# The last expert layer: eight lower-half splits go from GpSimd to VectorE, the gathers come in one run, and the combines come later

## The reference

```
scores = softmax(x_n @ gate_w.T)
i1, i2 = the two experts with the best scores
e(x)   = (silu(x @ W1[e].T) * (x @ W3[e].T)) @ W2[e].T
x     += scores[i1] * e_i1(x_n) + scores[i2] * e_i2(x_n) + shared(x_n)
```

## Time and profile before

| | |
|---|---|
| median of three runs | 1633.42 us |
| the profiled execution | 1632.18 us, its span 1630.4 us |
| TensorE busy | 1563.6 us, 96% of the span |
| VectorE, ScalarE, GpSimd busy | 1244.6, 1213.4, 1161.1 us |
| granted TensorE clock, mean | 0.993 of full speed |

### The profile page before, as it was taken

The page is one execution under the profiler, slowest core; times in us unless marked ns, Lnnn a source line. Parts: engine busy times, 40 slices in busy tenths (PEclk is TensorE's granted clock), DMA queues, the critical chain, the costliest instruction groups (busy, mean ns, idle before and its releaser), DMA issues. The chain is left out here.

```text
span 1630.4 us, 26805 instructions
## 1 busy us (share of the span) xinstructions
PE 1563.6 (96%) x9214; PEld 908.7 (56%) x9214; DVE 1244.6 (76%) x2330; ACT 1213.4 (74%) x1904; POOL 1161.1 (71%) x817
## 2 busy tenths in 40 slices
PE   3998899999999999999999999999999999998898
PEld 2565445555555555555555555555567566677665
DVE  7878787777777777777777777778787787977637
ACT  7876888988988989988988888887564543344442
POOL 0865888888888888888888898887565232556344
PEclk9999999999999999999999999999999999999999
DMA  9312879889779879879889788888103420000522
GB/s 307 126 53 47 135 145 166 151 144 185 147 145 184 150 145 179 151 151 173 149 152 170 146 144 156 156 147 145 32 1 76 113 55 1 1 1 14 114 95 84
DMA packets 641355, 197.10 MB, mean 121 GB/s; under 512 B 601531, under 2 KB 639046, under 8 KB 640966
## 3 DMA queue, kind: packets, MB, share of 16 engines
q1 hardware_dynamic: 636646, 188.19, 59.5%
q0 software_dynamic: 1536, 4.20, 0.8%
q10 hardware_dynamic: 3040, 3.02, 0.5%
HBM read 36.71 MB, written 10.22 MB: 29 GB/s over the span
## 5 line engine op out<-in xcount | busy, mean ns | idle before, releaser
L967 POOL TENSOR_TENSOR Pl<-Pm,Ph 128x1024 f16<-128x1024 f32 x256 | 545.5, 2131 | 44.4 <-ACT Ph L1308 43.9
L1298 ACT ACTIVATE Pm<-banks,nbias,s_scale 128x1024 f32<-128x1024 f32 x256 | 307.4, 1201 | 96.5 <-DVE nbias L1924 95.5
L1922 DVE TENSOR_REDUCE nmax<-banks 128x1 f32<-128x1024 f32 x256 | 311.6, 1217 | 87.3 <-PE banks L2454 86.9
L1308 ACT ACTIVATE Ph<-Pm 128x1024 f16<-128x1024 f32 x256 | 268.1, 1047 | 1.5
L946 POOL TENSOR_TENSOR rp_b<-rp_s,rope 128x512 f32<-128x512 f32 x128 | 162.8, 1272 | 98.4 <-ACT rp_s L1275 96.7
L1955 DVE SCALAR_TENSOR_TENSOR X<-banks,rinv,X 128x256 f32<-128x256 f32 x256 | 112.2, 478 | 113.2 <-PE banks L2454 113.2
L2452 PE MATMUL banks<-QK_hi 128*128 128x512 f16 x512 | 194.1, 379 | 1.6 <-DVE QK_lo L2013 0.9
L2452 PE MATMUL banks<-PT_hi,V_hi 128*128 128x512 f16 x512 | 194.0, 379 | 0.3 <-DMA PT_lo<-Pl 0.3
L2453 PE MATMUL banks<-QK_lo,QK_hi 128*128 128x512 f16 x512 | 194.0, 379 | 0.0
L2454 PE MATMUL banks<-QK_hi,QK_lo 128*128 128x512 f16 x512 | 194.0, 379 | 0.0
L2454 PE MATMUL banks<-PT_hi,V_lo 128*128 128x512 f16 x512 | 194.0, 379 | 0.0
(11 more groups left out here) (318 smaller groups left out, 3968.2 us busy)
## 6 DMA issues: line engine op xcount, KB each, us to landing
moe_raw<-in_L_ffn_W SPq DMA_DIRECT2D x48, 128.0 KB, 2.5
w_all<-in_L_attn_w_qkv SPq DMA_DIRECT2D x3, 2048.0 KB, 15.8
a_raw<-in_L_attn_w_qkv SPq DMA_DIRECT2D x24, 256.0 KB, 3.2
PT_hi<-Ph SPq DMA_TRANSPOSE x256, 3.4
PT_lo<-Pl SPq DMA_TRANSPOSE x256, 3.3
xs<-zeros SPq DMA_DIRECT2D x1, 2944.0 KB, 17.0
yd<-y_sb ACTq DMA_DIRECT2D x5, 512.0 KB, 2.9
raw_gu<-in_L_ffn_w_gate_up SPq DMA_DIRECT2D x2, 1024.0 KB, 7.2
```

The source lines that it names most:

```text
L967: nc.gpsimd.tensor_tensor(Pl[:, z % 4, :], Pm[:, k, :], Ph[:, z % 4, :], ALU.subtract).then_inc(pl_done.sem, 1)
L1298: nc.scalar.activation(Pm[:, k, :], two_banks[z % 2][:], ACT.Exp, bias=nbias[:, z:z + 1], scale=s_scale[:], accum_out=rsum[:, z:z + 1]).th ...
L1308: nc.scalar.activation(Ph[:, z % 4, :], Pm[:, (base * SLOTS + z) % 3, :], copy).then_inc(ph_done.sem, 1)
L1922: nc.vector.tensor_reduce(nmax[:, z:z + 1], two_banks[z % 2][:], AX, ALU.max, negate=True).then_inc(max_done.sem, 1)
```

## The change

Three tables and one loop are changed; no instruction computes anything else than before.

- `LO_BY_POOL` was 5 to 24 (20 units). It is now 5 to 12 and 21 to 24 (12 units). The lo of units 13 to 20 is now made by VectorE.
- The 16 gathers stood in pairs behind the lo of units 13 to 20. They now stand in one run behind the lo of unit 12 (`POOL_BEFORE_GATHER = 8`), ahead of the lo of unit 21.
- The combine of tile t stood in iteration 16+t. It now stands in iteration 19+t for tiles 0 to 5, and the combines of tiles 6 and 7 both stand in iteration 25.

```diff
-    COMBINE_AT = {16 + t: (t,) for t in range(TT)}
-    GATHER_BEHIND = {13 + t: (t,) for t in range(TT)}
-    LO_BY_POOL = tuple(range(5, NUB - 1))
+    COMBINE_AT = {19: (0,), 20: (1,), 21: (2,), 22: (3,), 23: (4,), 24: (5,), 25: (6, 7)}
+    LO_BY_POOL = (5, 6, 7, 8, 9, 10, 11, 12, 21, 22, 23, 24)
+    POOL_BEFORE_GATHER = 8
...
-                for i in LO_BY_POOL:
-                    expert_lo(i)
-                    gather(GATHER_BEHIND.get(i, ()))
+                expert_lo(LO_BY_POOL[:POOL_BEFORE_GATHER])
+                for i in range(2):
+                    pool.wait_ge(y_in[i].sem, 16 * XG // 2)
+                for t in range(TT):
+                    for k in range(TOPK):
+                        nc.gpsimd.indirect_dma_start(yg[:, t, k, :], None, yd,
+                                                     bass.IndirectOffsetOnAxis(pos[:, k, t:t + 1], 0)).then_inc(yg_in[t // 2].sem, 16)
+                expert_lo(LO_BY_POOL[POOL_BEFORE_GATHER:])
```

More of the change, by code:

```diff
@@ L1084, in scatter, with expert_lo @@
                         nc.gpsimd.indirect_dma_start(xs, bass.IndirectOffsetOnAxis(pos[:, k, t:t + 1], 0), row_tile(t), None).then_inc(xs_in.sem, 16)
[L1086 to L1099, removed]
+            def expert_lo(units):
+                for i in units:
+                    n = width(i)
+                    pool.wait_ge(mo_hi_done.sem, mo_hi_done.in_head(1, i + 1))
+                    nc.gpsimd.tensor_tensor(bT_lo[:, i % MT, 0:n], bo_h[:, i % 2, 0:n], bT_hi[:, i % MT, 0:n], ALU.subtract).then_inc(lo_pool.sem, 1)
             def last_experts(l):
```

## The result

The changed kernel took 1646.91 us (median of 4 runs, 1645.60 to 1647.91), the kernel before 1633.43 us beside it (4 runs, 1632.18 to 1634.13). The ratio is 1.0083 with a 95% interval of 1.0065 to 1.0100: 13.5 us or 0.83% slower, where I had forecast 1634.5 us and no change. The profiled execution took 1646.39 us with a span of 1644.3 us, 13.9 us more than before.

The account below looks back on a forecast made before the run. TensorE was taken to bound the kernel until 1622 us, then VectorE's lo(25) and adds. Terms 0 + 0 + 1.04 + 0 = +1.04 us on the median of 1633.42 gave 1634.5 us, range 1632.0 to 1636.8.

Parts of the forecast that it names:

- The gathers in one run: Sixteen gathers on GpSimd, from about 1575 to 1596 us, then some 10 us idle ahead of lo(21); worth zero.
- Both signs of being wrong: TensorE waiting for a lo or an add before 1620 us, or a span growing by more than 2 us.
- The third rival: Sixteen gathers in a row choke on GpSimd, lo(21) comes late, TensorE stands still 5.3 us: 1639.8 us; chance 3 in 100.
- The lo on VectorE: Lo of units 13 to 20 on VectorE, 0.61 us each in iterations 14 to 21; costs nothing.
- the margin of 0.06 us: VectorE in iterations 19 to 21, with lo and combine: 3.84 us of work in a period of 3.90.
- the cover of 1.3 us: Time to spare before TensorE waits for drained banks, with a lo ahead of the adds; hides an overrun of 1.3 us.
- the rule of the Trainium skill: A two-SBUF-input VectorE instruction and a GpSimd SBUF read share an interface; the later waits. Run might end 3.4 us later.
- The combines three iterations later: Zero up to tile 5; tiles 6 and 7 between product 25 and lo(25) on VectorE delay the end by 1.04 us.
- The sum: All terms for the span together: 0 + 0 + 1.04 + 0 = +1.04 us, from 1630.4 to 1631.4 us.
- the term of the combines: Combines of tiles 6 and 7 ahead of lo(25) on VectorE: +1.04 us, twelve adds following without a gap.

Follow-up runs that it names:

- e15: Changed kernel with a GpSimd pause of about 1.05 us ahead of the gathers of tiles 2, 4 and 6 only: 1634.56 us against 1633.27 before, ratio 1.0006.
- e9: Changed kernel, its run of sixteen gathers fetching and combining 64 of 128 rows each: 1647.20 us in one run.
- e8: Kernel before with a GpSimd pause of about 1 us ahead of each tile's two scatters but the first tile's: 1638.43 us against 1633.72, ratio 1.0032.
- e11: Kernel before with one more dense unit ahead of the sorted ones and a GpSimd pause behind every four scatters: 1630.05 us, ratio 0.9981.
- e1: Changed kernel with its gathers waiting in pairs for the upper halves of units 13 to 20: 1634.70 us against 1633.37 before, ratio 1.0007.
- e14: Changed kernel with a GpSimd pause of about 1.05 us ahead of each pair of gathers from the second tile on: 1635.04 us, ratio 1.0007.
- e4: Kernel before with the late combines alone and nothing else of the change: 1634.99 us against 1633.37, ratio 1.0011.
- e5: Changed kernel with its gathers in two groups of eight, behind the upper halves of units 13 and 17: 1636.01 us in one run, before 1633.72.
- e7: Changed kernel, its run of sixteen gathers fetching 128 of 256 columns, half the bytes: 1645.89 us in one run.

## Why the prediction was wrong

The gathers in one run: this step failed. I wrote that GpSimd is idle behind the run "and the long run delays nobody", and "This part is worth zero". The gathers themselves came as forecast (the first at 1575.32, about 1 us earlier than before; the last one done at 1595.1, forecast 1595.8), and the part cost 12 to 13 us. GpSimd was idle for 23 us ahead of lo(21) instead of 10, since lo(21) became due 12 us later. Both signs of being wrong that I had named came: TensorE waited 7.4 us for a lo before 1620 us, and the span grew by 13.9 us. I had asked who is queued behind the run on GpSimd, and who waits for the data. I had not asked what else the run goes past, and TensorE's signals were held up by it. The cost is not in the number of DMAs: with pauses the same sixteen cost nothing that shows (e15), and with half the rows each they cost as much as in the changed kernel (e9).

The third rival had the right sign and the right trigger, at 3 chances in 100, and the wrong mechanism. It let the gathers themselves slow down, with a threshold of 2.27 us each. They kept to 1.24 to 1.29 us, while TensorE stood still.

Against it I had set "twelve scatters in one run kept 1.26 to 1.46". That row is true, and it was the wrong question to it: I looked at how long the scatters took, not at what the others did beside them. The windows of 1516 to 1528 us and the two "remote" waits stood in the trace that I had. TensorE was idle there for 1.24 + 2.08 + 1.33 = 4.65 us. At most 3.41 of these belong to it: the first 1.24 us, a wait for VectorE, are there in e8 and e11 as well, although updates are prompt at that place.

The lo on VectorE: right that it costs nothing. In e1, with all of them, TensorE is busy for the whole of both windows. But the margin of 0.06 us did not hold in iteration 21, timeline of VectorE in the changed kernel:

```profile
1616.79 0.75 DVE L2277 SCALAR_TENSOR_TENSOR bo_h<-banks,l_pow,bo_s 128x512 f32<-128x512 f32 x1
...
1618.06 1.77 DVE L2260 SCALAR_TENSOR_TENSOR X<-yg,wk,X 128x256 f32<-128x256 f32 x2
...
1621.33 0.73 DVE L2277 SCALAR_TENSOR_TENSOR bo_h<-banks,l_pow,bo_s 128x512 f32<-128x512 f32 x1
```

Beside lo(21) on GpSimd (1618.29) the combine took 1.77 us instead of 1.00, and the iteration 4.54 us instead of 3.90. The 0.64 us were within the cover of 1.3 us, and the next iteration made them up (product 23 at 1624.59, two periods behind product 21).

I had weighed the rule of the Trainium skill, page "SBUF — State Buffer", section "Who interferes with whom", against the change. It cost nothing here: in the changed kernel no gather began while a lo was running, and they kept their 0.95 us. Where one does, the trace agrees with the rule. In e14 (GpSimd, then VectorE):

```profile
1587.74 1.38 POOL L1119 DMA_INDIRECT yg<-yd,pos  x1 [0.19 <-issue]
```

```profile
1587.55 0.68 DVE L2299 TENSOR_TENSOR bT_lo<-bo_h,bT_hi 128x512 f16<-128x512 f32 x1
```

The gather began with 0.49 us of the lo left and took 0.42 us longer than its neighbour (0.96 us).

The combines three iterations later: right. I had +1.04; e4 and the changed kernel both show 1.05 in the trace, and e1, which is the change without the long run, has 1634.70 us and a span of 1631.5, where I had forecast 1634.5 and 1631.4.

The sum therefore lacked one term, +12.1 us up to product 25: 10.07 us of TensorE standing still, and 2.0 us in its work around that. Most of the latter is the half clock: TensorE worked under it from 1599.49 to 1602.6, which costs an estimated 1.6 us (half of 3.1). Another 0.66 us come from the half clock at the end, behind a wait of TensorE of 2.1 us for an add; e1 and e4, with the same combines, have their twelve adds without a gap, so this is no part of the term of the combines.

## What to carry to other kernels

Before putting DMAs of GpSimd into one long run, look at what the other engines do beside the longest run that the trace already has. Where the waits name "remote", "an unknown queue" or "issue" on an engine that ought to wait for TensorE, compare the end of the matmul with the start of its waiter. Runs of four with 1 us of other work of GpSimd between were enough here beside the gathers, provided that nobody needs the data sooner; beside the last four scatters of e11 they were not quite enough.

## What the runs showed of the hardware

- TensorE's semaphore updates are late beside a run of indirect DMAs that GpSimd issues every 1.26 us. The first late one belongs to a matmul that ended 5.0 to 6.8 us after the run began, beside the fifth or sixth DMA (changed kernel 6.45, scatters of before 6.3, the groups of e5 6.8 and 5.0). Updates then come in order, up to 13 us late (changed kernel), and the last ones in a burst 0.8 to 3.5 us after GpSimd is done with the last DMA (3.0 in the changed kernel, 0.8 in e11, 3.5 in e9). VectorE's and ScalarE's recorded updates stay prompt. Neither half the bytes (e7) nor half the rows (e9) changes it.
- The count since the last pause is not the whole condition: in e11 the first late update belongs to a matmul that ended 1.6 us into the third group of four (1520.94), right behind a pause, while beside the gathers of e15 no group of four has one.
- TensorE itself slows down late in such a stretch: gaps of 1.03 and 1.52 us ahead of matmuls for which the profile names no wait (1589.60, 1591.72).
- By the Trainium skill, page "Perfetto Trace Analysis", section "Tensor Engine Instruction (MATMUL, LD_WEIGHTS)", two steps follow the modelled end of a matmul: PSUM acknowledges the last bytes, and the update travels to the other engines. The trace agrees in so far as the delay lies behind the matmul's row; in which of the two it lies, or in something ahead of both, no run here shows. Which resource the DMAs of GpSimd share with TensorE alone is open as well, and so is whether the recording of the profile takes part: every run here has a profiled span and clock beside its time, so none shows the kernel without it.
- A combine pair on VectorE took 1.77 us beside a lo on GpSimd (1618.06 and 1618.29 in the changed kernel), against 1.00 in the other iterations. An indirect DMA that GpSimd begins while a lo runs on VectorE takes longer, by less than what is left of the lo: 1.38 instead of 0.96 us with 0.49 us left (e14), 1.27 with 0.45 left (e5, 1578.27), 1.15 with 0.32 left.
